# A Macaron block on one core: the transposes of x moved ahead of the gate projection in both feed-forwards

## The chip, the cores and the metric

One NeuronCore of a Trainium2 chip runs the kernel in a single launch. The metric is the device time of one execution in microseconds (us). TensorE, VectorE (DVE in the profile), ScalarE (ACT), GpSimd (POOL) and SyncE (SP) have queues of their own, each worked off in order, and are kept in step by semaphores.

## The reference

Input x is 8 x 1024 x 256 float32. The block computes, with weights of 704 x 256 (gate and up), 256 x 704 (down) and four of 256 x 256:

```
x = x + 0.5 * ffn(layernorm(x))
x = x + attention(layernorm(x))     # 16 heads of 16, causal
x = x + 0.5 * ffn(layernorm(x))

ffn(x):  gate = fp4_linear(x, w_gate); y = fp4_linear(x, w_up)
         return fp4_linear(silu(gate) * y, w_down)
fp4_linear(x, w): both operands are quantized and dequantized in
         blocks of 16 along the last dimension (scale = max|.| / 6,
         values on the grid 0, 0.5, 1, 1.5, 2, 3, 4, 6), then x @ w.T
```

The same three feed-forward weights serve both feed-forwards.

## The kernel before, in words

The 8192 rows are 64 tiles of 128 rows, all of them resident in SBUF (`xs`). The program runs four stages one after the other: `feed_forward(0)` together with the preparation of the weights, the projection to q, k and v, the attention with its output projection, and `feed_forward(1)`, which also stores the result. The change is inside `feed_forward` (L576), so it acts in the first and the last stage.

A feed-forward is a software pipeline over the tiles, written out once for each engine in a function `step(i, par)`. `steps` (L638) calls it for i = -6 to 3 one by one, then in a hardware loop unrolled by six for i = 4 to 57, then one by one for 58 to 63. `ok(i)` drops work on tiles that do not exist. `done(eng, name, i)` (L625) makes an engine wait until the semaphore `name` has counted tile i of this phase. `early(i, first)` (L634) is true for the steps written out one by one from `first` to 2. Nobody reorders the work of an engine: it does exactly what its `step` lists.

What happens to one tile: VectorE takes the statistics of x (L712, L770), POOL makes rstd and shift, ScalarE normalizes (L919, `z`). Maxima of blocks of 16 (L730 for z, L735 for h), a reciprocal (L756), POOL's scaling (L793, L857), ScalarE's magnitudes (L869, L907) and VectorE's rounding (L741 and L762 for z, L675 and L681 for h) give the quantized values, which POOL scales back into `xq` (L818) and `hq` (L802). TensorE transposes them against an identity matrix (L987 for x, two instructions, L951 for h, six). ScalarE copies the transposed values to SBUF as a high part (L874, L880), VectorE subtracts that for a low part (L704, L665), and each product is three matmuls (high x high, low x high, high x low). Some of these temporaries share memory with attention buffers, so that the profile calls them `k_stack` or `q_stack`.

**TensorE's step i** (L975) in order: the up projection's PSUM bank 0 of tile i (six matmuls of 512 columns, L935); the two transposes of x of tile i + 1; banks 1 and 2 of tile i (six of 512 and six of 384 columns); the down projection of tile i - 3 (17 matmuls of 256 columns, L942 to L945); the six transposes of h of tile i - 2. "Up projection" stands here for gate and up together, which are one matrix of 1408 columns over three banks.

**VectorE's step i** (L707) in order: the low part of h of tile i - 3; statistics of tile i + 6; the product h = silu(gate) * up of tile i (L720), for which it waits for the third bank; the block maxima of z and h; the rounding u_z (L741) and u_h (L675); the **residual** of tile i - 3 (L670), x + 0.5 * down; the reciprocal; the rounding g_h and g_z; the low part of x of tile i + 2; the aggregation of the statistics.

**A shared bank.** `xd_ps` is one PSUM bank. Columns 0 to 255 (`xT_ps`) take the transposes of x, columns 256 to 511 (`down_ps`) take the down projection. So the transposes of x wait for the residual of tile i - 4 (L983), which is the last reader of the previous down projection and is made in VectorE's step i - 1.

Of the kernel before, what the change touches and what calls it, by code (L numbers as in the profile page):

```python
# [62 lines left out]
def passes(a, b):  # L63

    return (a[0], b[0]), (a[0], b[1]), (a[1], b[0])


def build(nc, x_in, wq_in, wk_in, wv_in, wo_in, wg_in, wu_in, wd_in, y_out):
    V, S, G, T = nc.vector, nc.scalar, nc.gpsimd, nc.tensor
    top = ExitStack()  # L70
    with top:
# [70 lines left out]
        def keep_busy(pe, to, weight, n):  # L142

            cols = to.shape[-1]
            for _ in range(n):
                last = T.matmul(to, weight[:, 0:P], weight[:, 0:cols], start=True, stop=True)
            return last
# [309 lines left out]
        A_RING, AHEAD = 4, 6  # L457
# [118 lines left out]
        def feed_forward(phase, store, begin=None, end=None, parts=0):  # L576
# [5 lines left out]
            with ExitStack() as ctx:  # L582
# [3 lines left out]
                def tmp(name, shape, dt=F32):  # L586
# [12 lines left out]
                            for a, n in ((0, HIDDEN), (2 * HIDDEN, DIM)))  # L599
                silu, h, u_z, g_z = (in_second[1][:, a:a + n] for a, n in  # L600
                                     ((0, HIDDEN), (HIDDEN, HIDDEN), (2 * HIDDEN, DIM), (2 * HIDDEN + DIM, DIM)))
# [19 lines left out]
                def ok(i):  # L621

                    return not isinstance(i, int) or 0 <= i < TILES

                def done(eng, name, i):  # L625

                    before = (base + 1) if name not in BOTH else phase * (TILES + 4) + 5
                    if isinstance(i, int):
                        i = min(i, TILES - 1)
                        if i + before <= 0:  # L630
                            return
                    eng.wait_ge(s[name], i + before)

                def early(i, first=1):  # L634

                    return isinstance(i, int) and first <= i <= 2

                def steps(name, eng, step, finish, each=None):  # L638

                    first, last, unroll = 4, TILES - 6, 6  # L640
                    for i in range(-AHEAD, first):
                        if name in begin and i + AHEAD < parts:
                            begin[name](eng, i + AHEAD)
                        if each:
                            each(i)
                        step(i, i % 2)
                    if each:
                        each(None)
                    with eng.Fori(0, (last - first) // unroll) as it:
                        for n in range(unroll):  # L650
                            step(it * unroll + (first + n), n % 2)
                    for i in range(last, TILES):
                        step(i, i % 2)
                        if name in end:
                            end[name](eng, i)
                    finish()

                with nc.Block() as block:
# [270 lines left out]
                    @block.tensor  # L929
                    def _(pe):  # L930
                        def up_project(n, buf):
                            cols = GU_BANKS[n]
                            for k in range(KD):
                                for m, (x, w) in enumerate(passes(xT, wguT)):
                                    last = T.matmul(gu_ps[:, n, 0:cols.stop - cols.start], x[:, buf, k * P:(k + 1) * P],  # L935
                                                    w[:, k, cols], start=k == 0 and m == 0, stop=k == KD - 1 and m == 2)
                            return last

                        def down_project(of, to):
                            for k in range(KH - 1):  # L940
                                for n, (x, w) in enumerate(passes(of, wdT)):
                                    T.matmul(to, x[:, k * P:(k + 1) * P], w[:, k, :], start=k == 0 and n == 0, stop=False)  # L942

                            T.matmul(to, of[0][:, (KH - 1) * P:KH * P], wdT_last[:, :], start=False, stop=False)  # L944
                            T.matmul(to, of[1][:, (KH - 1) * P:KH * P], wdT_last_hi[:, :], start=False,  # L945
                                     stop=True).then_inc(s["down"], 1)

                        def turn_h(i, to):
                            done(pe, "hq", i)
                            for k in range(KH):  # L950
                                last = T.matmul(to[:, k * P:(k + 1) * P], hq[:, k * P:(k + 1) * P], ident[:],  # L951
                                                is_transpose=True, start=k % 4 == 0, stop=True, skip_group_check=True)
                            last.then_inc(s["hT"], 1)

                        def finish():
                            done(pe, "resid", TILES - 4)
                            if not end:
                                keep_busy(pe, down_ps, wguT[0][:, 0, :], 16)
                            done(pe, "hT_lo", TILES - 3)
                            down_project(hT, down_ps)  # L960
                            turn_h(TILES - 2, hT_flat)
                            if end:
                                end["tensor"](pe, "turned")
                            else:
                                done(pe, "h", TILES - 1)
                                keep_busy(pe, gu_ps[:, 0, :], wguT[0][:, 0, :], 6)
                            done(pe, "g_h", TILES - 1)
                            turn_h(TILES - 1, hT_end_ps)
                            done(pe, "resid", TILES - 3)
                            done(pe, "hT_lo", TILES - 2)  # L970
                            down_project(hT, down_ps)
                            done(pe, "hT_lo", TILES - 1)
                            down_project(hT_end, down_end_ps)

                        def step(i, par):  # L975
                            if ok(i):

                                done(pe, "xT_lo", i)
                                done(pe, "silu", i - 1)
                                up_project(0, par)  # L980
                            if ok(i + 1):

                                done(pe, "resid", i - 4)  # L983
                                done(pe, "xT_lo", i)
                                done(pe, "xq", i + 1)
                                for k in range(KD):
                                    last = T.transpose(xT_ps[:, k * P:(k + 1) * P], xq[:, k * P:(k + 1) * P],  # L987
                                                       ident[:])
                                last.then_inc(s["xT"], 1)
                            if ok(i):  # L990
                                done(pe, "h", i - 1)
                                up_project(1, par).then_inc(s["gate"], 1)
                                up_project(2, par).then_inc(s["up"], 1)
                            if ok(i - 3):

                                done(pe, "resid", i - 4)
                                done(pe, "xT_hi", i + 1)
                                done(pe, "xT_lo", i + 1)
                                if isinstance(i, int) and i == 3:
                                    keep_busy(pe, down_ps, wguT[0][:, 0, :], 16)  # L1000
                                done(pe, "hT_lo", i - 3)
                                down_project(hT, down_ps)
                            if ok(i - 2):

                                done(pe, "hT_lo", i - 3)
                                turn_h(i - 2, hT_flat)

                        steps("tensor", pe, step, finish)

                    @block.sync  # L1010
# [1008 lines left out]
```

## Time and profile before

| | |
|---|---|
| median of 3 runs | 2041.84 us (2039.87 to 2044.87) |
| profiled execution | 2039.0 us |
| its span, first to last instruction | 2037.1 us |
| mean granted clock of TensorE | 0.998 |
| TensorE busy (matmuls) | 1973.6 us, 97% |
| VectorE busy | 1838.5 us, 90% |
| ScalarE busy | 1332.6 us, 65% |
| GpSimd busy | 1082.0 us, 53% |

How to read it: the span is that of one profiled execution, and the busy times are shares of it. Matmuls are pipelined, so a TensorE that is shown busy is one without pauses. The durations of two matmuls in a row overlap in the records, and what a matmul costs in a stream is the distance from its start to the next one's. The same holds for VectorE, whose instructions begin about 0.08 us before the recorded end of the one before when nothing holds them. The first feed-forward lies at about 30 to 495 us, the second at about 1600 to 2037 us.

### The profile page before, as it was taken

What the parts mean: (1) busy time and instruction counts of PE and PEld (TensorE: products, weight loads), DVE (VectorE), ACT (ScalarE), POOL (GpSimd) and SP (SyncE); (2) the same over time, 40 slices, a digit from 0 to 9 for tenths busy, and PEclk for the clock granted to TensorE, in tenths of its full rate; (3) what the DMA queues carried; (4) which work ended last, traced back from release to release, by engine and by line L of the source; (5) the groups of instructions that cost most, each with busy time, mean ns of one, the idle gap of its engine ahead of it and who ended that gap; (6) DMA issues with size and microseconds to landing.
All of it is one profiled execution on the core that took longest, in us unless ns stands there. A gap on an engine that the chain in (4) does not pass through costs nothing. (4 is left out here: it accounts for less than half of the span.)

```text
span 2037.1 us, 44334 instructions
## 1 busy us (share of the span) xinstructions
PE 1973.6 (97%) x13254; PEld 1299.4 (64%) x13254; DVE 1838.5 (90%) x4649; ACT 1332.6 (65%) x2324; POOL 1082.0 (53%) x1785
## 2 busy tenths in 40 slices
PE   5999999998999999999999999999988899999999
PEld 3888888887887333333333333333328788888888
DVE  7999999998788899999999999999937899999997
ACT  5445445444887788888888888888894354545453
POOL 5888888885664222221222222222222788888885
PEclk9999999999999999999999999999999999999999
DMA  6000000001876655555555554555335000000000
GB/s 215 16 0 0 0 0 0 0 0 37 268 227 214 135 149 136 135 138 137 139 139 149 144 132 138 138 138 138 109 96 199 6 21 20 16 21 21 15 21 27
DMA packets 134842, 185.03 MB, mean 91 GB/s; under 512 B 24928, under 2 KB 76512, under 8 KB 134368
## 3 DMA queue, kind: packets, MB, share of 16 engines
q1 hardware_dynamic: 132000, 182.11, 31.5%
q8 instruction: 74, 1.21, 0.2%
q10 hardware_dynamic: 2688, 1.05, 0.2%
q14 instruction: 80, 0.66, 0.1%
HBM read 113.90 MB, written 85.98 MB: 98 GB/s over the span
## 5 line engine op out<-in xcount | busy, mean ns | idle before, releaser
L1939 POOL TENSOR_SCALAR_AFFINE_SELECT diag_scores<-diag_scores 128x256 f32<-128x256 f32 (+1 forms) x320 | 148.3, 463 | 674.8 <-ACT diag_scores L1908 666.8
L1404 DVE CUSTOM_DVE_ANT_0 gu_ps<-gu_ps,mask_qk 128x256 f32<-128x256 f32 (+3 forms) x690 | 340.5, 529 | 49.7 <-PE gu_ps L1389 42.2
L1389 PE MATMUL gu_ps<-k_stack,q_stack 96*128 96x512 bf16 (+3 forms) x1050 | 318.0, 335 | 2.7 <-DVE part_max L1409 0.5
L1843 PE MATMUL gu_ps<-probs,v_group 128*17 128x512 f32 (+3 forms) x3072 | 310.8, 492 | 3.2 <-ACT probs L1914 2.0
L935 PE MATMUL gu_ps<-wguT_hi,ffn_xT_hi 128*128 128x512 f32 (+1 forms) x768 | 309.1, 402 | 1.2 <-DVE ffn_xT_lo L704 1.2
L935 PE MATMUL gu_ps<-wguT_hi,ffn_xT_lo 128*128 128x512 f32 (+1 forms) x768 | 287.6, 374 | 0.0
L935 PE MATMUL gu_ps<-wguT_lo,ffn_xT_hi 128*128 128x512 f32 (+1 forms) x768 | 287.3, 374 | 0.0
L1910 ACT ACTIVATE probs<-hT_ps 128x256 f32<-128x256 f32 (+2 forms) x320 | 259.7, 811 | 15.0 <-PE hT_ps L1819 14.7
L919 ACT ACTIVATE ffn_z<-xs,ffn_shift,ffn_rstd 128x256 f32 (+1 forms) x128 | 77.0, 602 | 293.2 <-POOL ffn_shift L786 293.2
L1910 ACT ACTIVATE probs<-av_ps 128x256 f32<-128x256 f32 (+2 forms) x320 | 263.6, 824 | 0.3
L1389 PEld LDWEIGHTS gu_ps<-k_stack,q_stack 96*128 96x128 bf16 x1050 | 95.4, 97 | 256.0 <-DVE part_max L1404 183.5
L1409 DVE TENSOR_REDUCE part_max<-gu_ps 128x1 f32<-128x512 f32 x360 | 235.2, 683 | 4.3 <-PE gu_ps L1389 1.1
L1819 PE MATMUL hT_ps<-q_stack,k_stack 98*128 98x512 bf16 (+3 forms) x768 | 229.1, 328 | 3.3 <-DMA k_stack<-k_parts 2.9
L802 POOL TENSOR_TENSOR ffn_hq<-ffn_g_h,ffn_nscale 128x704 f32<-128x704 f32 (+1 forms) x256 | 210.3, 842 | 6.3 <-PE hT_ps L951 3.2
L1819 PE MATMUL av_ps<-q_stack,k_stack 98*128 98x512 bf16 (+3 forms) x768 | 191.2, 326 | 2.1 <-ACT probs L1910 1.9
L942 PE MATMUL xd_ps<-wdT_hi,ffn_hT_hi 128*128 128x256 f32 x630 | 186.1, 295 | 3.9 <-DVE ffn_hT_lo L665 3.9
L857 POOL TENSOR_TENSOR q_stack<-k_stack,ffn_rec 128x704 f32<-128x704 f32 x128 | 178.2, 1392 | 7.1 <-DVE ffn_rec L756 6.8
L942 PE MATMUL xd_ps<-wdT_hi,ffn_hT_lo 128*128 128x256 f32 x630 | 176.0, 279 | 0.0
L942 PE MATMUL xd_ps<-wdT_lo,ffn_hT_hi 128*128 128x256 f32 x630 | 175.9, 279 | 0.0
L1404 DVE CUSTOM_DVE_ANT_0 xd_ps<-xd_ps,mask_qk 128x128 f32<-128x128 f32 (+3 forms) x334 | 154.8, 493 | 6.2 <-PE xd_ps L1389 5.6
L935 PEld LDWEIGHTS gu_ps<-wguT_hi,ffn_xT_lo 128*128 128x128 f32 x768 | 144.1, 188 | 22.8
L935 PEld LDWEIGHTS gu_ps<-wguT_hi,ffn_xT_hi 128*128 128x128 f32 x768 | 144.6, 188 | 19.6 <-DVE ffn_xT_lo L704 1.9
(221 smaller groups left out, 4893.0 us busy)
## 6 DMA issues: line engine op xcount, KB each, us to landing
q_stack<-q_parts SPq DMA_DIRECT2D x192, 128.0 KB, 3.4
k_stack<-k_parts SPq DMA_DIRECT2D x192, 128.0 KB, 3.6
o_all<-o_sb SPq DMA_DIRECT2D x64, 256.0 KB
q_parts<-qkv_parts SPq DMA_DIRECT2D x32, 384.0 KB, 2.8
k_parts<-qkv_parts SPq DMA_DIRECT2D x32, 384.0 KB, 4.3
v_ones<-qkv_vst SPq DMA_DIRECT2D x16, 544.0 KB, 3.9
v_group<-v_ones SPq DMA_DIRECT2D x32, 272.0 KB, 4.3
xs<-in_L_attn_x SPq DMA_DIRECT2D x8, 1024.0 KB, 8.1
```

The costliest lines, as they stand in the source:

```text
L802: last = G.tensor_tensor(blocks(hq[:, to:to + n]), blocks(g_h[:, of:of + n]), spread(nscale[:, par, of // BLK:(of + n) // BLK]), ALU.mult)
L857: G.tensor_tensor(blocks(v_h[:, par, :]), blocks(h[:]), spread(rec[:, OF_H]), ALU.mult).then_inc(s["v_h"], 1)
L919: S.activation(z[:, 1 - par, :], x_tile(i + 5), ACT.Identity, bias=shift[:], scale=rstd[:]).then_inc(s["z"], 1)
L935: last = T.matmul(gu_ps[:, n, 0:cols.stop - cols.start], x[:, buf, k * P:(k + 1) * P], w[:, k, cols], start=k == 0 and m == 0, stop=k == K ...
L942: T.matmul(to, x[:, k * P:(k + 1) * P], w[:, k, :], start=k == 0 and n == 0, stop=False)
L1389: mm = T.matmul(out[:, e, :], qs[0:STACK, h0 + e, t * P:(t + 1) * P], ks[0:STACK, h0 + e, c * CHUNK:c * CHUNK + w], start=True, stop=True)
L1404: last = V.tensor_tensor_reduce(out=ps[:, e * w:(e + 1) * w], in0=ps[:, e * w:(e + 1) * w], in1=mask_qk[:, CHUNK - w:CHUNK], scale=1.0, sc ...
L1409: last = V.tensor_reduce(part_max[:, h0:h0 + per, t, c], ps[:, 0:per * w].rearrange("p (h w) -> p h w", h=per), AX.X, ALU.max)
L1819: mm = T.matmul(scores[pair][:, e, at:at + w], ks[0:STACK_MAX, h, t * P:(t + 1) * P], qs[0:STACK_MAX, h, (j + 1) * CHUNK - w:(j + 1) * CHUNK],
L1843: mm = T.matmul(o_ps[h * VPAD:h * VPAD + VCOLS, CHUNK - w:CHUNK], vs[:, t, h, :], probs[:, h // 2, i % 2, h % 2, at:at + w], start=first, ...
L1910: S.activation(probs[:, pair, i % 2, :, first:w], scores[pair][:, :, first:w], ACT.Exp, scale=DH ** -0.5).then_inc(s[pr], 1)
L1939: G.affine_select(out=block_of, in_=block_of, compare_op=ALU.is_ge, fill=MASKED, base=0, pattern=[[0, 2], [0, count], [1, P]], channel_mul ...
```

## The change

In TensorE's step, the transposes of x with their three waits become a function `turn_x`. In steps up to 2 it is called where it stood, behind bank 0. In all others, those of the hardware loop among them, it is called ahead of bank 0, which is right behind the transposes of h that end the step before. The instructions of the other engines, VectorE's statistics of x (L712, L770) among them, are as they were.

```diff
--- before.py
+++ after.py
@@ -973,13 +973,7 @@
                             down_project(hT_end, down_end_ps)
 
                         def step(i, par):
-                            if ok(i):
-
-                                done(pe, "xT_lo", i)
-                                done(pe, "silu", i - 1)
-                                up_project(0, par)
-                            if ok(i + 1):
-
+                            def turn_x():
                                 done(pe, "resid", i - 4)
                                 done(pe, "xT_lo", i)
                                 done(pe, "xq", i + 1)
@@ -987,6 +981,16 @@
                                     last = T.transpose(xT_ps[:, k * P:(k + 1) * P], xq[:, k * P:(k + 1) * P],
                                                        ident[:])
                                 last.then_inc(s["xT"], 1)
+
+                            if ok(i + 1) and not early(i, -AHEAD):
+                                turn_x()
+                            if ok(i):
+
+                                done(pe, "xT_lo", i)
+                                done(pe, "silu", i - 1)
+                                up_project(0, par)
+                            if ok(i + 1) and early(i, -AHEAD):
+                                turn_x()
                             if ok(i):
                                 done(pe, "h", i - 1)
                                 up_project(1, par).then_inc(s["gate"], 1)
```

## Rows read from the trace of the kernel before

**Rows 1.** Stretches of the run: per engine its busy us and instructions, then clock, DMA share, GB/s.

```profile
60.00:100.00 40.00, 37.08 (x238) 32.81 (x237) 37.69 (x72) 18.34 (x34) 32.81 (x58) 1.00 0.00 1
...
200.00:300.00 100.00, 100.00 (x628) 88.95 (x627) 98.29 (x192) 50.19 (x89) 87.32 (x147) 1.00 0.00 0
```

**Rows 2.** Waits in 100 to 450 us: who waited for whom, total us, times, longest.

```profile
PEld xd_ps L942 <- issue: 7.8, 44, 0.2
```

**Rows 3.** Timeline of TensorE, one step: start us, duration us, engine, line, operation, tiles.

```profile
306.66 0.36 PE L942 MATMUL xd_ps<-wdT_hi,ffn_hT_hi 128*128 128x256 f32 x1
...
308.63 0.28 PE L945 MATMUL xd_ps<-wdT_last_hi,ffn_hT_lo 128*128 128x256 f32 x1
308.75 0.82 PE L951 MATMUL hT_ps<-ident,ffn_hq 128*128 128x128 f32 x6
309.32 0.48 PE L935 MATMUL gu_ps<-wguT_hi,ffn_xT_hi 128*128 128x512 f32 x1
...
310.79 0.38 PE L987 MATMUL xd_ps<-ident,ffn_xq 128*128 128x128 f32 x2
310.93 0.47 PE L935 MATMUL gu_ps<-wguT_hi,ffn_xT_hi 128*128 128x512 f32 x1
311.24 0.39 PE L935 MATMUL gu_ps<-wguT_lo,ffn_xT_hi 128*128 128x512 f32 x1
...
313.25 0.34 PE L935 MATMUL gu_ps<-wguT_hi,ffn_xT_lo 128*128 128x384 f32 x1
```

**Rows 4.** Timeline of POOL, the same step.

```profile
307.64 0.62 POOL L818 TENSOR_TENSOR ffn_xq<-k_stack,ffn_nscale 128x256 f32<-128x256 f32 x1
```

**Rows 5.** Timeline of VectorE, the same step.

```profile
305.56 0.96 DVE L665 TENSOR_TENSOR ffn_hT_lo<-hT_ps,ffn_hT_hi 128x768 fp32r<-128x768 f32 x1
...
306.87 0.89 DVE L720 TENSOR_TENSOR k_stack<-k_stack,gu_ps 128x704 f32<-128x704 f32 x1
...
309.93 0.41 DVE L670 SCALAR_TENSOR_TENSOR xs<-xd_ps,xs 128x256 f32 x1
...
313.68 0.89 DVE L720 TENSOR_TENSOR k_stack<-k_stack,gu_ps 128x704 f32<-128x704 f32 x1
```

**Rows 6.** Timeline of all engines at the beginning of the first phase.

```profile
70.39 0.42 DVE L670 SCALAR_TENSOR_TENSOR xs<-xd_ps,xs 128x256 f32<-128x256 f32 x1
...
70.77 0.48 PE L935 MATMUL gu_ps<-wguT_hi,ffn_xT_hi 128*128 128x512 f32 x1
...
75.23 0.89 DVE L720 TENSOR_TENSOR k_stack<-k_stack,gu_ps 128x704 f32<-128x704 f32 x1
...
78.28 0.41 DVE L670 SCALAR_TENSOR_TENSOR xs<-xd_ps,xs 128x256 f32 x1
```

**Rows 7.** Timeline of VectorE: residuals 57 and 58 of phase one, 1, 57, 58, 59 of phase two.

```profile
459.73 0.41 DVE L670 SCALAR_TENSOR_TENSOR xs<-xd_ps,xs 128x256 f32<-128x256 f32 x1
...
467.11 0.42 DVE L670 SCALAR_TENSOR_TENSOR xs<-xd_ps,xs 128x256 f32<-128x256 f32 x1
...
1620.29 0.41 DVE L670 SCALAR_TENSOR_TENSOR xs<-xd_ps,xs 128x256 f32 x1
...
2001.85 0.41 DVE L670 SCALAR_TENSOR_TENSOR xs<-xd_ps,xs 128x256 f32<-128x256 f32 x1
...
2005.81 0.89 DVE L720 TENSOR_TENSOR k_stack<-k_stack,gu_ps 128x704 f32<-128x704 f32 x1 [0.37 <-PE gu_ps L935]
...
2008.33 0.41 DVE L670 SCALAR_TENSOR_TENSOR xs<-xd_ps,xs 128x256 f32<-128x256 f32 x1
...
2015.15 0.41 DVE L670 SCALAR_TENSOR_TENSOR xs<-xd_ps,xs 128x256 f32<-128x256 f32 x1
```

**Rows 8.** Timeline of TensorE: transposes of x that start from a wait.

```profile
60.97 0.41 PE L987 MATMUL xd_ps<-ident,ffn_xq 128*128 128x128 f32 x2 [0.46 <-POOL ffn_xq L818]
61.13 0.48 PE L935 MATMUL gu_ps<-wguT_hi,ffn_xT_hi 128*128 128x512 f32 x1
```

**Rows 9.** Timeline of TensorE: sixteen matmuls behind the longest idle of this stretch.

```profile
66.27 2.15 PE L146 MATMUL xd_ps<-wguT_hi 128*128 128x256 f32 x16 [2.47 <-DVE ffn_xT_lo L704]
```

## The prediction, made before the changed kernel ran

> **What bounds the kernel now.** I read the table of stretches first, then the waits of the first feed-forward, then one step of TensorE and one of VectorE in the timeline, since the change only reorders TensorE's work within a step. In 200 to 300 us the two are busy 100% and 98% of the time at the full granted clock [rows 1], so neither has room to absorb a wait. What TensorE still loses there is short: 44 waits of about 0.18 us each before the down projection [rows 2], which begins 0.14 us after VectorE's hT_lo ends (305.56 + 0.96 = 306.52, matmul at 306.66) [rows 3, 5].
>
> One step lasts 6.81 us: h to h on VectorE is 306.87 to 313.68, and residual to residual over the whole first phase is (459.73 - 78.28) / 56 = 6.81 [rows 5 to 7]. Within the step the reader should see five moments. TensorE's down projection ends at 308.63 + 0.28 = 308.91; the six transposes of h start at 308.75; up projection bank 0 starts at 309.32; the two transposes of x start at 310.79; the last matmul of the up projection starts at 313.25 and ends at 313.59 [rows 3]. VectorE multiplies h 0.09 us after that, at 313.68, and it makes the residual of the earlier tile at 309.93, ending 310.34 [rows 5].
>
> That last pair matters. The residual's data are ready at 308.91, yet it runs a microsecond later, because it stands behind the multiply, two block maxima and two rounding instructions in VectorE's queue: 3.06 us from the start of h (306.87) to its own start [rows 5]. Today nobody feels this. The transposes of x write the same PSUM bank as the down projection's result, so they wait for the residual, but at 310.79 it has been over for 0.45 us, while TensorE did bank 0.
>
> **The change part by part.** Nothing is added or removed; no DMA and no instruction of another queue moves. In steps 3 to 62 of each phase, two transposes and their three waits move ahead of bank 0's six matmuls. The order in the steps up to 2 is as before.
>
> - *Switching.* The first matmul behind a run of transposes is followed 0.31 us later (310.93 to 311.24), the others 0.23 us: six matmuls and the gap to the transposes take 309.32 to 310.79 = 1.47 = 0.31 + 5 x 0.232 [rows 3]. Eight transposes in one run leave one such place instead of two: -0.08 us a step.
> - *The waits for xq and xT_lo.* The xq that POOL has finished at 307.64 + 0.62 = 308.26 is that of the tile to be transposed or a later one, and it stands before the transposes of h begin [rows 4]; xT_lo was already waited for by bank 0. Cost nothing. If that cover went (xq 1.1 us later), TensorE would wait on POOL instead.
> - *The wait for the residual.* TensorE reaches the transposes at about 309.32, and the residual ends at 310.34 [rows 3, 5]. Behind this wait stand all 18 matmuls of the up projection, the down projection and the next transposes of h; VectorE's multiply waits for the up projection, and the next residual stands behind that multiply. That closes a loop of one step. Its length, from the residual's end: 0.14 us until the transposes start (the same as hT_lo to the down projection); 0.16 us to the first matmul (60.97 to 61.13, the one place where these transposes start from a wait [rows 8]; without one it is 0.14); then 1.47 + (313.25 - 310.93 = 2.32) - 0.08 = 3.71 us to the last matmul's start; 0.34 us for it; 0.09 us to h; 3.06 us to the residual and 0.41 us for it. Sum 7.91 us against 6.81: **+1.10 us a step**.
>
> The trace holds one unplanned instance of this loop. At the beginning of the phase bank 0 of a step starts at 70.77, just as the first residual ends (70.39 + 0.42 = 70.81). The multiply follows at 75.23 and the next residual at 78.28, 7.89 us after the first [rows 6]. That step costs nothing more under the change, as does its twin in the second phase.
>
> Other covers: hT_lo ends at 306.52, 3.0 us after the residual of the step before it (310.34 - 6.81 = 303.53), and the down projection would come 4.2 us behind that residual, so the present 0.18 us wait vanishes inside the longer loop. The down projection's end (308.91, 2.04 us after h) still precedes the residual (3.06 us after h).
>
> How many steps: the residuals of tiles 0 to 58 release the transposes of steps 4 to 62. In the first phase residual 1 to residual 57 are 56 intervals: 56 x 7.91 = 443.0 us against 459.73 - 78.28 = 381.5 [rows 6, 7], +61.5. The interval after them is 7.38 us as it stands (459.73 to 467.11), because VectorE begins the attention's preparation in it; I put it at nothing. In the second phase the same 56 take 1620.29 to 2001.85 = 381.6: +61.4. The next two take 6.48 and 6.82 us (2001.85, 2008.33, 2015.15); VectorE has no x work left in them and comes from h to the residual in 2.52 us (2005.81 to 2008.33) where it took 3.06, so the loop is 7.37 us there: +0.9 and +0.55 [rows 7]. Later steps have no transposes of x. Together **+124.4 us**. The profiled execution took 2039.0 us; 2039.0 + 124.4 = 2163.4. The median shown is 2.8 us above that execution, so I predict 2166.2.
>
> Bounds of the one unseen thing, a step in which this wait ends last every time. Below: if VectorE's end reached TensorE in 0.03 us, not 0.14, the loop is 7.80 us, 114 x 0.11 = 12.5 us less, 2153.7. Above: if each restart cost TensorE another 0.08 us (the price of a change of kind, once more) and VectorE 0.05 us, 8.04 us, 14.8 us more, 2181. I take 7.91, since the instance from 70.39 to 78.28 lies within 0.02 us of it.
>
> A rule to be weighed: in the rows the transposes of x start at 310.79, after the residual's end at 310.34 and not beside it [rows 3, 5], and the code makes them wait for it although they write other columns of xd_ps than it reads. The Trainium skill ("PSUM — Partial Sum Buffer", PSUM bank collisions raise a hardware error) tells one to guard PSUM by bank and quadrant and not by address; by it the wait can't be dropped while both share a bank, and the sum is 2166; were the wait no more than one on an address, the first rival's 2032 would follow.
>
> **The rivals.**
>
> *Faster: the residual is early enough.* If the residual were over when the transposes of h are through, only the saved switch would be left: 2 x 60 x 0.08 = 9.6 us off, 2032. The deciding point is the residual's end against 309.32. It would have to come 1.02 us earlier, and VectorE is 98% busy with a fixed order [rows 1, 5]. Chance 2%.
>
> *No change: the wait is there but VectorE has slack before h.* TensorE's idle time would be paid by slack in VectorE between the residual and h: 310.34 to 313.68. VectorE is busy throughout, but TensorE is not the only one to set h; if it were VectorE that set h and the up projection ended more than 1 us before it, the time would stay 2042. The rows show 0.09 us between the up projection's end and h. Chance 1%.
>
> *Slower by more: a second wait in the loop.* If hq or xq on POOL (87% busy [rows 1]) or ACT's casts came late in the new rhythm, say by 0.3 us a step, 114 steps would add another 34 us: 2200. All of these hang on VectorE's results, which move along with the loop, and the pause lies in front of h, so they gain time. Chance 4%.
>
> *Slower by far: the clock falls.* TensorE would stand still about 1.0 us in each step. At half clock the 3.7 us of columns in the loop would double: 114 x 3.7 = 422 us more, some 2590. Against it: after 2.47 us of idling the next 16 matmuls took 2.15 us, 0.12 us apart, the rate of the undisturbed ones, and the stretch of 60 to 100 us around it has a granted clock of 1.00 [rows 1, 9]. The Trainium skill ("TensorE: Matmul & The Clock Gate", Why this matters for your kernels) says that idle gaps between bursts of matmuls return the engine to its lower clock; by it this change would be a danger, and the trace's longer gap, which did not lower it, speaks against that here. Chance 1%.
>
> **How the numbers follow.** The forecast case has 92%, the four rivals 2, 1, 4 and 1%. The range of the forecast is that of the bounds, 2153 to 2181; it holds some nine tenths of the forecast case and needs nothing of the rivals. Faster by over 0.3% (about what a measurement of this kernel can tell from no change) is the first rival, 0.02; within it the second, 0.01; slower the rest, 0.97.
>
> **What would show it.** In the changed profile: a step of 7.9 us in both phases; a wait of TensorE for the residual's line before the transposes of x, about 1.0 us long, in some 110 steps; VectorE idle about 1.2 us before h, released by TensorE's up projection; the multiply 4.4 us after the residual's end; VectorE's share down to 85% in the feed-forward, the clock at 1.00; attention's time unchanged. Wrong would be a step under 7.7 us (VectorE's order has slack that I don't see), one above 8.1 (a second wait, which the waits would name), or no wait for the residual at all.

## The result and the profile after

The changed kernel takes 2171.41 us (median of 6, 2170.32 to 2174.96) against 2041.22 us (median of 6) for the kernel before: ratio 1.0643, 95% interval 1.0632 to 1.0655, 130 us slower. Predicted were 2166.2 us and a range of 2153 to 2181.

The table of stretches of the changed kernel, to be read beside [rows 1]: per engine busy us and instructions for TensorE, its weight loads, VectorE, ScalarE, POOL, then granted clock, DMA share, GB/s.

```profile
60.00:65.00 5.00, 3.87 (x11) 3.11 (x12) 4.86 (x7) 2.60 (x5) 3.89 (x8) 0.66 0.00 0
60.00:100.00 40.00, 35.62 (x214) 31.80 (x215) 33.36 (x65) 17.66 (x32) 30.90 (x53) 0.96 0.01 1
200.00:300.00 100.00, 87.19 (x547) 78.11 (x546) 82.32 (x164) 42.70 (x76) 75.50 (x126) 1.00 0.00 0
...
1660.00:1680.00 20.00, 16.52 (x88) 14.10 (x87) 16.31 (x34) 7.87 (x15) 14.89 (x26) 0.83 0.00 1
1750.00:1850.00 100.00, 86.61 (x533) 76.74 (x534) 82.46 (x164) 42.38 (x76) 74.79 (x124) 1.00 0.05 18
```

In 200 to 300 us TensorE is busy 87 us where it was 100, and VectorE 82 where it was 98. The clock there is 1.00. Two short stretches, at the beginning of each phase, are at a lower mean clock; they come back below.

The waits of 100 to 500 us (engine and line that waited, who ended it, total us, times, longest):

```profile
ACT ffn_z L919 <- POOL ffn_shift L786: 121.6, 50, 2.6
ACT k_stack L896 <- PE gu_ps L935: 83.0, 50, 1.7
PEld xd_ps L981 <- issue: 64.9, 50, 1.4
DVE k_stack L720 <- ACT k_stack L896: 57.9, 43, 1.4
POOL ffn_dscale L840 <- DVE ffn_amax L735: 57.5, 51, 1.4
PE xd_ps L981 <- DVE xs L670: 53.3, 50, 1.1
```

The longest wait, ScalarE for POOL's shift, was there before (129.0 us in 51 steps of 100 to 450 us) and is slack of an engine that is busy 42 us in 100. What is new: the wait of [rows 2], before the down projection, is gone from the list, and in its place TensorE stands before the transposes of x, 53.3 us in 50 steps, until VectorE's residual is there. The same microsecond shows up on every engine: VectorE before h 57.9 us in 43 steps, POOL 57.5 us before its scales. VectorE's wait is credited here to ScalarE's silu, because silu and the up projection's last bank end close together; in other steps the same wait is credited to TensorE (next fence, 314.43). One loop of waits looks like four separate problems in a list of waits.

One turn of that loop in the timeline, TensorE and then VectorE (start, duration, operation, idle time and what ended it), beside [rows 3, 5]:

```profile
300.15 0.82 PE L951 MATMUL hT_ps<-ident,ffn_hq 128*128 128x128 f32 x6
302.01 0.43 PE L981 MATMUL xd_ps<-ident,ffn_xq 128*128 128x128 f32 x2 [1.03 <-DVE xs L670]
302.20 0.47 PE L935 MATMUL gu_ps<-wguT_hi,ffn_xT_hi 128*128 128x512 f32 x1
302.51 0.39 PE L935 MATMUL gu_ps<-wguT_lo,ffn_xT_hi 128*128 128x512 f32 x1
...
305.89 0.34 PE L935 MATMUL gu_ps<-wguT_hi,ffn_xT_lo 128*128 128x384 f32 x1
...
308.07 0.82 PE L951 MATMUL hT_ps<-ident,ffn_hq 128*128 128x128 f32 x6
```

```profile
301.46 0.41 DVE L670 SCALAR_TENSOR_TENSOR xs<-xd_ps,xs 128x256 f32 x1
301.79 0.52 DVE L756 RECIPROCAL ffn_rec<-ffn_dscale 128x60 f32<-128x60 f32 x1
...
306.32 0.89 DVE L720 TENSOR_TENSOR k_stack<-k_stack,gu_ps 128x704 f32<-128x704 f32 x1 [1.34 <-ACT k_stack L896]
...
309.37 0.41 DVE L670 SCALAR_TENSOR_TENSOR xs<-xd_ps,xs 128x256 f32 x1
...
314.43 0.89 DVE L720 TENSOR_TENSOR k_stack<-k_stack,gu_ps 128x704 f32<-128x704 f32 x1 [1.39 <-PE gu_ps L935]
...
317.48 0.41 DVE L670 SCALAR_TENSOR_TENSOR xs<-xd_ps,xs 128x256 f32 x1
```

The residual ends at 301.46 + 0.41 = 301.87. The transposes start at 302.01 (+0.14), the first matmul at 302.20 (+0.19), the last at 305.89 (+3.69) and ends at 306.23; h starts at 306.32 (+0.09) and the next residual at 309.37 (+3.05). Residual to residual is 7.91 us. The one after that is 8.11 us (309.37 to 317.48), to which the runs return.

### The profile page after: what moved, and what is told of

The parts are those of the page before. It is cut to its first block and busy times, and to the rows that moved or that the text cites. A ratio compares the mean times of both kernels' runs of the same rounds, so it can differ in the third digit from the quotient of the medians.

```text
span 2170.4 us, 44316 instructions
## 1 busy us (share of the span) xinstructions
PE 1986.7 (92%) x13254; PEld 1312.7 (60%) x13254; DVE 1826.9 (84%) x4649; ACT 1332.6 (61%) x2324; POOL 1082.8 (50%) x1785
## 5 line engine op out<-in xcount | busy, mean ns | idle before, releaser
L935 PE MATMUL gu_ps<-wguT_hi,ffn_xT_hi 128*128 128x512 f32 (+1 forms) x768 | 300.1, 391 | 0.0
L720 DVE TENSOR_TENSOR k_stack<-k_stack,gu_ps 128x704 f32<-128x704 f32 x128 | 113.6, 888 | 169.7 <-ACT k_stack L896 125.5
L896 ACT ACTIVATE k_stack<-gu_ps 128x704 f32<-128x704 f32 x128 | 97.3, 760 | 209.4 <-PE gu_ps L935 209.4
L942 PE MATMUL xd_ps<-wdT_hi,ffn_hT_hi 128*128 128x256 f32 x630 | 176.3, 280 | 3.0 <-DVE ffn_hT_lo L665 3.0
L981 PE MATMUL xd_ps<-ident,ffn_xq 128*128 128x128 f32 x256 | 55.4, 298 | 127.7 <-DVE xs L670 121.7
```

What stands on the lines that cost most here:

```text
L896: S.activation(silu[:], gate_ps, ACT.Silu).then_inc(s["silu"], 1)
```

## The experiments

In all of them other ways of reading the result were kept open: that it is the order of the transposes, or POOL's xq, or the clock, or VectorE's amount of work that costs, and not the loop through the residual.

**1. The wait taken away by its reason, the order kept.** `x_in_free_bank`, on the changed kernel:

```diff
# in short: turn_x, xT_high and xT_low take xT_at(i) in place of xT_ps
-xT_ps, down_ps, ... = xd_ps[:, 0:DIM], xd_ps[:, DIM:2 * DIM], ...
+def xT_at(i):
+    return xd_ps[:, 0:DIM] if isinstance(i, int) and i <= 3 \
+        else hT_ps[:, 1, DIM:2 * DIM]
...
 def turn_x():
-    done(pe, "resid", i - 4)
+    if isinstance(i, int) and i == 3:
+        done(pe, "hT_lo", 0)
...
 def xT_low(i, par):
     done(dve, "xT_hi", i)
+    if not isinstance(i, int) or i > 3:
+        done(dve, "hT_hi", i - 4)
```

> The changed order, but from tile 4 on the transposed x lies in the unused columns of the second PSUM bank of hT, so the transposes of x no longer wait for the residual (for tile 4 alone they wait for the low part of h of tile 0, and VectorE's low part of x waits for ScalarE's high part of h, which keeps the bank's readers apart). Loop theory: TensorE never stands before the transposes of x, the step falls back to 6.8 us or to 0.04 us under it (one change of kind less for TensorE, halved because the present loop runs over two steps), time 2034 to 2042. Order theory (it is the order itself, or POOL's xq, that costs): the order is the same, so the time stays within 10 us of 2171. Clock theory: no forecast of its own, since the pauses go too.

Measured: 2038.10 us (median of 10) against 2040.42 us, ratio 0.9989 [0.9979, 0.9998]. All 130 us are gone although the transposes of x stand where the change puts them. The order theory falls, and with it POOL's xq, for which the transposes still wait at the same place. TensorE's timeline, transposes of h, then of x:

```profile
303.77 0.82 PE L956 MATMUL hT_ps<-ident,ffn_hq 128*128 128x128 f32 x6
304.43 0.38 PE L988 MATMUL hT_ps<-ident,ffn_xq 128*128 128x128 f32 x2
```

The transposes of x follow those of h by 0.66 us and show no wait. From residual 1 to residual 57 a step takes (460.02 - 82.36) / 56 = 6.74 us in the first phase, against 6.81: 0.07 us less, where 0 to 0.04 were expected for the saved change of kind. The edit has a price of its own: in step 3 of each phase TensorE stands 4.96 and 5.27 us for VectorE's low part of h of tile 0, a wait that the edit added, and in the first phase the matmuls after it run at the lower clock level (0.54 granted on average from 65 to 70 us).

**2. The same wait at two other lengths.** `residual_one_earlier` and `residual_two_earlier`, on the changed kernel, move two lines of VectorE's step:

```diff
 # residual_one_earlier: ahead of u_h; residual_two_earlier: ahead of u_z
+if ok(i - 3):
+    residual(i - 3, down_ps)
 if ok(i - 1) and not early(i):
     ...
     round_up(i - 1, 1 - par)
-if ok(i - 3):
-    residual(i - 3, down_ps)
```

> The changed kernel with VectorE's residual moved ahead of one instruction, the rounding u_h (0.80 us from start to start). Loop theory: h to residual falls from 3.06 to 2.26 us, the down projection's end at 2.13 us is still before it, so the loop is 7.1 us: 114 steps x 0.80 = 91 us less than 2171, 2080. Order theory and clock theory: TensorE does the same in the same order; within 10 us of 2171 (order), or a jump to some value not in proportion to 0.80 us a step (clock).

> The changed kernel with the residual moved ahead of two instructions, the roundings u_z and u_h. Loop theory: the residual would be ready to run at 1.93 us after h, but the down projection ends at 2.13 us, and VectorE then stands for 0.2 us itself; a step of 7.0 us, 0.9 us less in 114 steps, 2068. So the second instruction gives back only 0.1 us a step of its 0.33. If the down projection did not matter, the step would be 6.8 and the time 2043. Order theory: 2171.

Measured: 2081.24 us, ratio 1.0201 [1.0184, 1.0218], and 2058.88 us, ratio 1.0088 [1.0071, 1.0104]. The first instruction gives back 90 us (91 expected), the second 22 (12 expected). VectorE's timelines, first with one instruction, then with two passed over:

```profile
304.50 0.89 DVE L720 TENSOR_TENSOR k_stack<-k_stack,gu_ps 128x704 f32<-128x704 f32 x1 [0.54 <-ACT k_stack L896]
...
306.42 0.42 DVE L741 SCALAR_TENSOR_TENSOR k_stack<-av_ps,q_stack 128x256 f32<-128x256 f32 x1
306.75 0.41 DVE L670 SCALAR_TENSOR_TENSOR xs<-xd_ps,xs 128x256 f32 x1
307.08 0.88 DVE L675 SCALAR_TENSOR_TENSOR ffn_u_h<-av_ps,q_stack 128x704 f32<-128x704 f32 x1
...
311.61 0.89 DVE L720 TENSOR_TENSOR k_stack<-k_stack,gu_ps 128x704 f32<-128x704 f32 x1 [0.54 <-ACT k_stack L896]
```

```profile
304.97 0.89 DVE L720 TENSOR_TENSOR k_stack<-k_stack,gu_ps 128x704 f32<-128x704 f32 x1 [0.21 <-ACT k_stack L896]
...
306.10 0.88 DVE L735 TENSOR_REDUCE ffn_amax<-k_stack 128x44 f32<-128x704 f32 x1
307.03 0.42 DVE L670 SCALAR_TENSOR_TENSOR xs<-xd_ps,xs 128x256 f32 x1
...
311.90 0.89 DVE L720 TENSOR_TENSOR k_stack<-k_stack,gu_ps 128x704 f32<-128x704 f32 x1 [0.22 <-ACT k_stack L896]
```

With one, h to residual is 2.25 us (304.50 to 306.75), and h to h 7.11. With two it is 2.06 us (304.97 to 307.03), and h to h 6.93: the residual starts 0.14 us after its predecessor would let it, because the down projection's last matmul ends at 306.88, as TensorE's timeline of the same run shows (by the queue alone it would have started 0.79 us after the maxima of h, at 306.10 + 0.79 = 306.89):

```profile
306.60 0.28 PE L945 MATMUL xd_ps<-wdT_last_hi,ffn_hT_lo 128*128 128x256 f32 x1
```

So the price follows the length of the loop and stops where the down projection becomes the later of the two, at 2.06 us and not at the 2.13 that I had worked out; the reckoned step was 7.0.

**3. The control.** `before_residual_one_earlier`, the same edit on the kernel before.

> The kernel before, with the residual moved ahead of u_h as in the run residual_one_earlier. Loop theory: nobody waits for the residual in the kernel before, so the time is that of the kernel before within 0.3%: 2041. If an earlier residual were good for some other reason, this run would be faster too, by up to 90 us.

Measured: 2041.72 us, ratio 1.0005 [0.9995, 1.0014]. An earlier residual is worth 90 us with the change and nothing without it.

**4. Is it VectorE's amount of work?** The diff is one line, on three kernels:

```diff
-V.bn_stats(stats[:], x_tile(i + 6)).then_inc(s["stats"], 1)
+V.bn_stats(stats[:], x_tile(i + 6)[:, 0:8]).then_inc(s["stats"], 1)
```

> The changed kernel, with VectorE's statistics of x taken over 8 of the 256 columns of a row (it leaves out the other 248, for its time alone). That instruction lasts 0.42 us; about 0.25 us of it should go. Loop theory: the statistics lie between the residual and h, where VectorE stands 1.4 us anyway, so the step stays 7.92 and the time 2171. Load theory (VectorE's amount of work bounds the changed kernel): 0.25 x 124 = 31 us less, 2140.

> x_in_free_bank, with the same short statistics (248 of 256 columns left out). There VectorE's queue is the bound as x_in_free_bank_low_first suggests, TensorE needing some 6.6 us a step: 0.15 to 0.25 us less in 114 steps, 2038 - 17 to 28, 2010 to 2021. If TensorE bounds already: 2038.

> The kernel before, with the same short statistics (248 of 256 columns left out). VectorE at 98% and TensorE's two changes of kind a step: some 0.1 to 0.15 us less in a step of 6.81, 2041 - 11 to 17, 2024 to 2030. So the same saving on VectorE should be worth most where the transposes of x stand early and wait for nobody, less in the order of before, nothing in the changed kernel.

Measured: 2169.32 us, ratio 1.0634 [1.0618, 1.0650]; 2035.66 us, ratio 0.9976 [0.9966, 0.9986]; 2039.66 us, ratio 0.9999 [0.9990, 1.0008]. The load theory falls for the changed kernel. But the two others gained next to nothing either, against what I expected of them: nothing on the kernel before, and 2.4 us on x_in_free_bank where 17 to 28 were expected. Those 2.4 us do not come from the step, which stays at (458.24 - 80.66) / 56 = 6.74 us; residual 1 already comes 1.7 us earlier (80.66, not 82.36). VectorE's timeline of the kernel before with short statistics shows why:

```profile
306.29 0.96 DVE L665 TENSOR_TENSOR ffn_hT_lo<-hT_ps,ffn_hT_hi 128x768 fp32r<-128x768 f32 x1
307.16 0.16 DVE L712 BATCH_NORM_STATS2 ffn_stats<-xs 128x6 f32 x1
307.60 0.89 DVE L720 TENSOR_TENSOR k_stack<-k_stack,gu_ps 128x704 f32<-128x704 f32 x1 [0.27 <-ACT k_stack L896]
```

The instruction shrank to 0.16 us and h took the time as a wait of 0.27 us. The statistics stand between hT_lo and h, and h waits in any case for ScalarE's silu and the up projection. I read the step of the kernel before as a loop over two steps: from the end of hT_lo TensorE runs through the down projection, the transposes and the up projection without a pause until h (306.52 to 313.68 in [rows 3, 5], 7.16 us), and VectorE from h without a pause to the end of the next hT_lo (306.87 to 306.52 + 6.81 = 313.33, 6.46 us), together two steps of 6.81. That the two stretches add up to two steps is true of any two moments of a repeating step and shows nothing; what speaks for the reading is that neither engine pauses on its stretch beyond the short wait for hT_lo of [rows 2], and that VectorE's statistics lie outside it and are worth nothing. It is argued and not shown.

**5. Shortening that other loop.** `x_in_free_bank_low_first`, on x_in_free_bank:

```diff
-if ok(i - 3) and not early(i - 1, 2):     # first in VectorE's step
-    hT_low(i - 3, hT, hT_flat)
...
+if ok(i - 2) and not early(i, 2):
+    hT_low(i - 2, hT, hT_flat)
 if ok(i + 2) and not (early(i, -2) and i == -2):
     xT_low(i + 2, par)
```

The first hT_low of `finish` goes with it, and so does the added wait in xT_low.

> x_in_free_bank, and VectorE makes the low part of h of tile i - 2 at the end of step i, ahead of the low part of x and the aggregation, not at the beginning of the next step. Loop theory: with the residual out of the loop the step of 6.75 us hangs on the old loop over two steps, from hT_lo through the down projection, the transposes, the up projection and h. hT_lo comes about 0.4 us earlier in it, so the loop is 0.2 us shorter, and VectorE's own work (some 6.6 us) becomes the bound: 114 steps x 0.1 = 11 us less than 2038, 2027, 2020 if nothing of VectorE waits. If VectorE's work alone bounds x_in_free_bank already: 2038.

Measured: 2040.62 us, ratio 0.9999 [0.9990, 1.0007]: no gain. Its timeline of VectorE:

```profile
299.69 0.41 DVE L673 SCALAR_TENSOR_TENSOR xs<-xd_ps,xs 128x256 f32 x1
...
301.20 0.41 DVE L762 SCALAR_TENSOR_TENSOR k_stack<-av_ps,k_stack 128x256 f32<-128x256 f32 x1
301.56 0.96 DVE L668 TENSOR_TENSOR ffn_hT_lo<-hT_ps,ffn_hT_hi 128x768 fp32r<-128x768 f32 x1
302.43 0.41 DVE L706 TENSOR_TENSOR ffn_xT_lo<-hT_ps,ffn_xT_hi 128x256 fp32r<-128x256 f32 x1
302.76 0.17 DVE L772 BATCH_NORM_AGGREGATE ffn_aggr<-ffn_stats 128x2 f32<-128x6 f32 x1
303.07 0.43 DVE L712 BATCH_NORM_STATS2 ffn_stats<-xs 128x6 f32 x1
303.42 0.87 DVE L720 TENSOR_TENSOR k_stack<-k_stack,gu_ps 128x704 f32<-128x704 f32 x1
...
306.45 0.41 DVE L673 SCALAR_TENSOR_TENSOR xs<-xd_ps,xs 128x256 f32 x1
```

VectorE waits for TensorE no more in this step: h starts at 303.42, 0.08 us ahead of the recorded end of the statistics (303.50), as it does when only the queue holds it. The queue alone takes 6.76 us from residual to residual (299.69 to 306.45). The edit has itself made that queue longer: the statistics, which the code makes wait for the aggregation, now stand right behind it and start 0.31 us after it (302.76 to 303.07), where in x_in_free_bank the low part of h stood there and started 0.08 us after it (300.61 to 300.69). So the run shortened one thing and lengthened another, and doesn't decide what bounds x_in_free_bank.

A bound that I had not weighed lies closer, TensorE's own queue. In `free_bank_short_statistics` VectorE waits before h (16.0 us for silu, 43 times, in 100 to 450 us), so its queue is not what holds the step of 6.74 us. TensorE there goes without a pause from the second matmul of one down projection (300.19) to the second of the next (306.87), which is 6.68 us. Whatever VectorE saves, the step can fall by some 0.06 us at most, 7 us in 114 steps. The expectations of 11 to 28 us for this run and for the short statistics on x_in_free_bank put TensorE's need at 6.6 us or left it out. Which part of the last 0.06 us is the loop over two steps and which VectorE's queue stays open.

**6. What the forecast lacked: the turn of the hardware loop.** In the changed kernel every sixth interval is 8.11 us. `changed_unroll2` and `before_unroll2`:

```diff
-first, last, unroll = 4, TILES - 6, 6
+first, last, unroll = 4, TILES - 6, 2
```

> The changed kernel, with the hardware loop over tiles 4 to 57 unrolled by two and not by six: 27 turns of the loop and not 9 in each phase. In the changed kernel every sixth interval between residuals is 8.11 us, the others 7.92, so a turn of the loop costs 0.2 us when it lies in the loop of waits. Loop theory: 18 turns more in each of two phases, 36 x 0.2 = 7 us more, 2178. If the 0.2 us has another cause (refetching code of the long body), the time stays or falls.

> The kernel before with the same unrolling by two. There, a long interval of 6.92 us is followed by a short one of 6.73, so a turn of the loop is hidden in part: between 0 and 4 us more than 2041, clearly less than the 7 us of the changed kernel.

Measured: 2178.84 us, 7.4 us over the changed kernel (ratio to before 1.0678 [1.0663, 1.0692]), and 2041.38 us, ratio 1.0004 [0.9995, 1.0013]. In the first of them every second interval between residuals is 8.11 us, the others 7.92. A turn of the hardware loop costs 0.2 us inside the loop of waits and nothing measurable outside it (0.3 us for 36 turns more). The rival, the fetching of a long body's code, would have made the time stay or fall. What the 0.2 us consist of stays open.

**7. Step 3.** `changed_step3_as_before`:

```diff
-if ok(i + 1) and not early(i, -AHEAD):
+if ok(i + 1) and not (early(i, -AHEAD) or isinstance(i, int) and i == 3):
     turn_x()
 ...
-if ok(i + 1) and early(i, -AHEAD):
+if ok(i + 1) and (early(i, -AHEAD) or isinstance(i, int) and i == 3):
     turn_x()
```

> The changed kernel, with step 3 of both phases in the order of before (the transposes of tile 4 behind bank 0). In the changed kernel TensorE stands 2.6 and 2.9 us there for xq of tile 4 and shows half the clock for some 4 us after it; the first residuals come 0.4 and 1.4 us later than before relative to the preceding stage. Loop theory with this addition: granted clock 1.00 from 60 to 65 us again, time 2169 to 2171, the steps unchanged at 7.92. If the waits in steps 4 to 62 also cost clock, it would not show here.

Measured: 2170.02 us, 1.4 us under the changed kernel, which is inside the spread of both; the steps are unchanged (7.94 us on average in the first phase in both). What it was about is seen in the changed kernel's TensorE at the beginning of the first phase:

```profile
61.13 0.44 PE L981 MATMUL xd_ps<-ident,ffn_xq 128*128 128x128 f32 x2 [2.56 <-POOL ffn_xq L818]
61.30 0.71 PE L935 MATMUL gu_ps<-wguT_hi,ffn_xT_hi 128*128 128x512 f32 x1
61.80 0.63 PE L935 MATMUL gu_ps<-wguT_lo,ffn_xT_hi 128*128 128x512 f32 x1
...
64.79 0.40 PE L935 MATMUL gu_ps<-wguT_hi,ffn_xT_lo 128*128 128x512 f32 x1
65.03 0.39 PE L935 MATMUL gu_ps<-wguT_hi,ffn_xT_hi 128*128 128x512 f32 x1
```

After 2.56 us of standing, matmuls of 512 columns start 0.43 us apart (61.80 and on), from 64.79 to 65.03 0.24: the lower clock level (1.2 GHz; 512 columns in 0.43 us) and the upper one (2.4 GHz). From 60 to 65 us the granted clock is 0.66 on average. With step 3 as before it reads 1.00 there, but 0.66 in the next 5 us, behind the older wait of 2.47 us before sixteen matmuls [rows 9], which then took 3.47 us. From 60 to 100 us both kernels have a granted clock of 0.96. So in the first phase the edit moved the stretch at the lower level and didn't save it, which is why it is worth so little.

**8. The version with both lessons.** `free_bank_step3_as_before` is x_in_free_bank with step 3 as in experiment 7, tile 4 in the old bank too, and without the extra wait for hT_lo in turn_x.

```diff
-    return xd_ps[:, 0:DIM] if isinstance(i, int) and i <= 3 \
+    return xd_ps[:, 0:DIM] if isinstance(i, int) and i <= 4 \
...
-    if not isinstance(i, int) or i > 3:
+    if not isinstance(i, int) or i > 4:
```

> x_in_free_bank, with the transposes of tile 4 left behind bank 0 and in the old bank, so that TensorE doesn't stand for xq of tile 4 in step 3 (in x_in_free_bank it loses clock there: 0.91 granted from 60 to 100 us). Expected: granted clock 0.97 or more from 60 to 100 us, and 1 to 4 us less than 2038: 2034 to 2037, the only version here that is clearly under the kernel before.

Measured: 2033.77 us (median of 5), ratio 0.9960 [0.9946, 0.9973], 0.4% faster than the kernel before, and 4.3 us under x_in_free_bank. The time came as expected, the clock did not: it is 0.96 from 60 to 100 us, where 0.97 or more was expected, since behind the wait of 2.47 us the sixteen matmuls ran at the lower level here too. What the edit removes is the longer standing of 4.96 and 5.27 us in step 3, which ended with the low part of h and not, as the expectation says, with xq. The step is 6.74 us, (457.51 - 80.07) / 56, the same as without the mended step 3, and residual 1 comes at 80.07 and not 82.36. The two profiled executions lie only 1.3 us apart (2033.83 and 2035.15), so the 4.3 us between the medians are not traced in full.

## Why the prediction was right

**The direction and the mechanism held in steps 4 to 62.** TensorE reaches the transposes early (308.07 plus 0.66, against 309.78 for the residual's end in the same turn), waits about 1.1 us, and everything queued behind it moves. The multiply comes 4.45 us after the residual's end (4.44 reckoned), the next residual 3.05 us after that (3.06), and the step of the first phase is 7.91 to 7.92 us (7.91). VectorE idles 1.34 us before h where 1.2 were forecast, and is busy 82% where 85 were. Of the rivals, the early residual falls by the wait itself, and the slack before h by the step, which is 1.10 us longer. TensorE waits for the residual 121.7 us in 115 steps over the whole run:

```profile
PE xd_ps L981 <- DVE xs L670: 121.7, 115, 1.2
```

**The covers held.** The wait for hT_lo vanished, the down projection's end stayed ahead of the residual, xq and ScalarE's casts cost nothing in steps 4 to 62, so there was no second wait. x_in_free_bank keeps to the rule of the Trainium skill ("PSUM — Partial Sum Buffer", PSUM bank collisions raise a hardware error), to guard by bank and quadrant and not by address: it gives the transposed x another bank, whose readers are kept in order by waits that are over in the steady step, and the wait goes with all its price. What dropping the wait within the shared bank would do, no run here shows.

**The sum was 9 us short** of the profiled difference (span 2170.4 - 2037.1 = 133.3, against 124.4). By the medians the forecast was 5 us short (2171.4 against 2166.2), because it added 2.8 us for a profiled execution that was below its median; the changed kernel's was 0.8 us above its own. By the residuals' starts: the 56 intervals of the first phase took 444.6 us (78.95 to 523.54) where 443.0 were reckoned, those of the second 448.0 us (1685.79 to 2133.76), also 443.0. Missing in the sum were the turns of the hardware loop, 9 in each phase at 0.2 us, 3.6 us together (experiment 6). The prediction had taken the loop's length from one step inside a body. In the second phase every step is 0.06 us longer still, 7.98:

```profile
1806.46 0.43 PE L981 MATMUL xd_ps<-ident,ffn_xq 128*128 128x128 f32 x2 [1.05 <-DVE xs L670]
1806.65 0.48 PE L935 MATMUL gu_ps<-wguT_hi,ffn_xT_hi 128*128 128x512 f32 x1
...
1810.41 0.34 PE L935 MATMUL gu_ps<-wguT_hi,ffn_xT_lo 128*128 128x384 f32 x1
```

First to last matmul of the up projection is 3.76 us here and 3.69 in the first phase (302.20 to 305.89). With 56 steps that is 3 to 4 us. The obvious suspects are the stores of the result, which run only in this phase (0.05 of the DMA engines' time from 1750 to 1850 us), but the trace speaks against them: a step at the beginning of the phase, with no transfer (1678.44 to 1682.20, DMA share 0.00), already takes 3.76 us, and so do the seven behind it, with a store in them (share about 0.20) or without one (3.75 to 3.77 us). Nor is it all due to the change: matmuls of 512 columns start 0.233 us apart in the second phase of both kernels, and 0.231 (before) and 0.229 us (changed) in the first. Before, the step was 6.81 us in both phases all the same. The cause stays open; the step of the prediction that missed it is that the loop's length was read in one phase and used for both.

The rest is small: 0.4 us before the first residual, 0.25 us on residual 0 to 1 in each phase (it is 8.14 and 8.19 us, where the prediction had "nothing more"), 1.4 us between the phases, part of which is step 3. The last two of the intervals reckoned in the second phase took 1.45 us more, as forecast. So the range held while two of its terms were missing: its upper end of 2181 came from dearer restarts, of which only 0.03 us a step was seen (0.19 us to the first matmul, not 0.16), made good by 3.69 us for the matmuls where 3.71 were reckoned, and not from the turns of the hardware loop or from a slower phase. That the missing terms fitted into room kept for something else was luck.

**A step that failed, with little effect: step 3.** The prediction put the wait for xq at nothing. That holds in the steady state and not in step 3, where xq of tile 4 comes late and TensorE stood 2.56 and 2.91 us.

**The fourth rival was argued from one row.** [rows 9] showed sixteen matmuls in 2.15 us after 2.47 us of standing, and the prediction took it that such a gap does not lower the clock. In free_bank_step3_as_before the same gap is followed by the same matmuls at the lower level:

```profile
66.59 3.56 PE L146 MATMUL xd_ps<-wguT_hi 128*128 128x256 f32 x16 [2.47 <-DVE ffn_xT_lo L709]
```

The same place stands in both phases of six of the runs (the kernel before, its three variants, changed_step3_as_before and this one), after a gap of 2.44 to 2.48 us each time. The sixteen matmuls took 2.15 us in four of the twelve cases, 2.6 and 2.9 us in two, and 3.45 to 3.66 us in six.

The conclusion was still right for the steps that matter. Gaps of 1.1 us in every step left the clock at 1.00 (200 to 300 and 1750 to 1850 us). The Trainium skill ("TensorE: Matmul & The Clock Gate", Why this matters for your kernels) warns of idle gaps between bursts of matmuls, and its row speaks of gaps above a certain length. The prediction left that out and so called the change a danger by it. The traces agree for gaps of 2.5 to 2.9 us, some of them, and none of the gaps of 1.1 us did harm.

## What to carry to other kernels

Before moving an instruction ahead in an in-order queue, list its waits and ask for each when it is satisfied at the new place, and what stands behind it: a wait that was over by 0.45 us became one of 1.1 us in 114 steps. The wait closed a loop from VectorE to TensorE and back, and such a loop costs its whole length in every step, whatever an engine's busy share says; its length can be added up from the trace before. Where the wait comes from a shared buffer and not from data, a place of its own is the edit to look for: here it turned +130 us into -2 us, and -7 us with step 3 left alone. And read the length of such a loop in every phase, and at the turn of a hardware loop too, before multiplying it by the number of steps.

## What the runs showed of the hardware

Two things I had not expected. A turn of the hardware loop costs 0.2 us (8.11 against 7.92 us, 36 more turns made 7.4 us) and is hidden where no wait of one step's length passes through it (36 more turns made 0.3 us). And the same gap of about 2.47 us in the same place was followed by the upper clock level in some cases (2.15 us for sixteen matmuls) and by the lower in others (3.45 to 3.66 us), even in the two phases of one execution of free_bank_step3_as_before (3.56 and 2.15 us), so that one execution is no proof that a gap is harmless.
